# Weighing the second half of the heads as three fp32r products in an attention and mixture-of-experts kernel

## The reference, cut to what matters

```python
# x: (32, 128, 128), ctx_512: (32, 128, 64); 16 heads of width 64
qh = layernorm(x) @ Wq;  kh = ctx @ Wk;  vh = ctx @ Wv          # per head
attn = softmax(qh @ kh.T / 8)
x = x + tanh(g_xattn) * ((attn @ vh) joined over heads @ Wo + bo)
h = layernorm(x)
# 32 experts of width 64, 8 taken per token out of 2 of 4 groups, and a shared MLP
x = x + tanh(g_ffn) * (sum over taken experts of w * mlp_e(h) + mlp_shared(h))
```

## Time and profile before

| | |
|---|---|
| median of 3 runs | 668.14 us (667.93 to 668.69) |
| the profiled execution's own time | 665.33 us |
| its span | 663.5 us |
| PE busy | 649.6 us, 98% |
| DVE busy | 498.2 us, 75% |
| ACT busy | 365.1 us, 55% |
| POOL busy | 287.1 us, 43% |
| attention part | from the start to about 353 us |
| granted PE clock | full speed in all of the 40 slices |

### The profile page before, as it was taken

How to read it: one execution, slowest core, us unless ns; L and a number is a source line. 1 busy time by engine, 2 the same in 40 slices (tenths; PEclk the granted TensorE clock), 3 DMA queues, 4 the chain that set the end, 5 groups by cost and what they waited for, 6 DMA issues and landing times.

```text
span 663.5 us, 13627 instructions
## 1 busy us (share of the span) xinstructions
PE 649.6 (98%) x3668; PEld 472.3 (71%) x3668; DVE 498.2 (75%) x1330; ACT 365.1 (55%) x689; POOL 287.1 (43%) x317
## 2 busy tenths in 40 slices
PE   8999999999999999999999999999999999999997
PEld 5656666666666666676657878788887878788785
DVE  6989857767677775867786969968695977869564
ACT  3564556555465654656455555555655555555553
POOL 4222313233132331314302656566565656656654
PEclk9999999999999999999999999999999999999999
DMA  8323323232332323223226635272645535364640
GB/s 184 100 65 82 94 63 82 62 82 70 80 81 63 85 63 83 71 70 91 52 67 166 157 89 132 77 174 79 163 112 121 130 78 141 85 159 112 147 128 16
DMA packets 63244, 65.58 MB, mean 99 GB/s; under 512 B 26080, under 2 KB 41568, under 8 KB 63200
## 3 DMA queue, kind: packets, MB, share of 16 engines
q1 hardware_dynamic: 63200, 65.07, 39.4%
HBM read 61.64 MB, written 2.88 MB: 97 GB/s over the span
## 4 chain that ended last, share of the span: by engine, by line
PE 65%; DMA 9%; issue 8%; SPq 6%; DVE 6%; POOL 4%; ACT 1%; DVEq 0%; POOLq 0%; ACTq 0%
PE bank L1131 15%; PE bank L1132 14%; PE bank L1133 14%; PE bank L1207 7%; DMA inverse_bc<-inverse_dram 5%; POOL halves L501 4%; PE bank L1231 3%; PE bank L1167 3%; DMA inverse_dram<-inverse 2%; SPq L293 2%; PE bank L1187 2%; SPq L301 1%; DVE row_max L776 1%; DVE area L790 1%; PE bank L1196 1%
## 5 line engine op out<-in xcount | busy, mean ns | idle before, releaser
L501 POOL TENSOR_TENSOR halves<-area,halves 128x512 fp32r<-128x512 f32 x135 | 175.2, 1298 | 141.6 <-ACT halves L634 137.6
L647 ACT ACTIVATE area<-bank 128x512 f32<-128x512 f32 x136 | 81.4, 598 | 112.4 <-PE bank L1133 111.4
L587 ACT ACTIVATE area<-bank 128x512 f32<-128x512 f32 x128 | 69.5, 595 | 116.7 <-PE bank L1196 116.7
L1091 DVE TENSOR_TENSOR bank<-area,bank 128x512 f32<-128x512 f32 x128 | 88.5, 691 | 52.8 <-PE bank L1133 52.7
L1207 PE MATMUL bank<-area,ctx_keys 128*65 128x512 f32 (+1 forms) x256 | 124.7, 599 | 0.9 <-ACT u_odd L535 0.9
L1131 PE MATMUL bank<-x2t_hi,w_hi 128*128 128x512 f32 x272 | 110.1, 405 | 0.1
L1132 PE MATMUL bank<-x2t_hi,w_lo 128*128 128x512 f32 x272 | 107.1, 394 | 0.0
L1133 PE MATMUL bank<-x2t_lo,w_hi 128*128 128x512 f32 x272 | 106.2, 391 | 0.0
L447 POOL TENSOR_TENSOR ctx_hi<-ctx_raw,ones_col 128x128 fp32r<-128x128 f32 x32 | 20.4, 639 | 193.3 <-DMA ctx_raw<-ctx_t 193.3
L776 DVE TENSOR_REDUCE row_max<-bank 128x4 f32<-128x512 f32 x128 | 81.6, 679 | 25.8 <-PE bank L1167 21.5
L634 ACT ACTIVATE halves<-area 128x512 fp32r<-128x512 f32 x136 | 85.0, 626 | 16.8 <-DVE area L1099 16.3
(11 more groups left out here) (128 smaller groups left out, 1086.2 us busy)
## 6 DMA issues: line engine op xcount, KB each, us to landing
wbc<-rows_dram SPq DMA_DIRECT2D x128, 256.0 KB, 4.2
inverse_bc<-inverse_dram SPq DMA_DIRECT2D x64, 256.0 KB, 3.9
w_raw<-experts SPq DMA_DIRECT2D x32, 102.0 KB, 2.0
ctx_raw<-ctx_t SPq DMA_DIRECT2D x32, 64.0 KB, 1.8
ctx_keys<-ctx_nat SPq DMA_DIRECT2D x32, 64.0 KB, 2.0
out<-area SPq DMA_DIRECT2D x7, 256.0 KB, 3.9
max_rows<-max_t SPq DMA_DIRECT2D x64, 4.0 KB
area<-wq_t SPq DMA_DIRECT2D x1, 512.0 KB, 4.7
```

Of the source, the lines that this page charges most:

```text
L501: nc.gpsimd.tensor_tensor(hid_lo[:, u % SLOTS, :], hid[:, u % HIDS, :], raw(hid_hi[:, u % SLOTS, :]), ALU.subtract).then_inc(hidlo_ready, 1)
L587: nc.scalar.activation(probs_t[:, k, :, :], st_ps[q][:].rearrange("p (h n) -> p h n", h=4), ACT.Exp)\
L647: nc.scalar.activation(silu_g[:, u % 2, :], gate_ps[u % 2][:], ACT.Silu).then_inc(silu_ready, 1)
L1091: nc.vector.tensor_tensor(up_ps[u % UPS][:], silu_g[:, u % 2, :], up_ps[u % UPS][:], ALU.mult)\
```

## The change

In tiles t = 3 to 27 (25 of 32: the last tile of the first chunk and all of the loop) the two fp32 matmuls of half 1 are replaced by six fp32r matmuls of 512 columns on high and low halves. The halves come from new operations: ACT copies the exponentials of half 1 to `p_hi` (two operations of 128x512 a tile), DVE subtracts to form `p_lo` (two, both inputs in SBUF), POOL splits the context into `keys_hi` and `keys_lo` (128x192 each). They lie in tiles that are free in this time: `x2t_hi`, `x2t_lo` and the tails of `w_hi`, `w_lo`. DVE's part stands after `residual` and the statistics, ahead of `ln_apply`. In even steps ACT's part stands ahead of both `u_out` of half 0, in odd steps behind them.

```diff
+HALVED_FROM = CB - 1
+        p_hi = [x[:, 1, :] for x in (x2t_hi, x2t_lo)]
+        tail = slice(WCOLS - 2 * 3 * CD, WCOLS)
+        p_lo = [x[:, 0, :] for x in (x2t_hi, x2t_lo)]
+        keys_hi, keys_lo = (w[:, tail].rearrange("p (s n) -> p s n", s=2) for w in (w_hi, w_lo))
+        def halved_weights(b, first, last):
+            return not last and (not first or b == CB - 1)
 # POOL
+            def split_keys(b, t, c):
+                pool.wait_ge(keys_in[b], 16 * c + 16)
+                wait(pool, u_done, 4 * (t - 1) if not isinstance(t, int) or t > HALVED_FROM + 1 else 0)
+                nc.gpsimd.tensor_tensor(keys_hi[:, b % 2, :], ctx_keys[:, b, :], ones_col[:].broadcast_to([P, 3 * CD]),
+                                        ALU.mult).then_inc(keyshi_ready, 1)
+                pool.wait_ge(keyshi_ready, t + 1 - HALVED_FROM)
+                nc.gpsimd.tensor_tensor(keys_lo[:, b % 2, :], ctx_keys[:, b, :], raw(keys_hi[:, b % 2, :]), ALU.subtract)\
+                    .then_inc(keyslo_ready, 1)
...
+                    if halved_weights(b, first, last):
+                        split_keys(b, t, c)
                     split_weights(b % 2, t, 2 * c + b // 2, NB if last else t + CB)
 # ACT
+            def probs_high(t):
+                act.wait_ge(exp_ready, 4 * t + 4)
+                for q in range(2):
+                    nc.scalar.activation(p_hi[q], probs_t[:, 2 + q, :, :].rearrange("p h n -> p (h n)"), ACT.Copy)\
+                        .then_inc(phi_ready, 1)
...
+                    if b % 2 == 0 and halved_weights(b, first, last):
+                        probs_high(t)
                     u_out(t, b % 2, 0, 0)
                     if b % 2 == 1 and not last:
                         g_high(2 * c + 2 + b // 2, b // 2)
                     u_out(t, b % 2, 0, 1)
+                    if b % 2 == 1 and halved_weights(b, first, last):
+                        probs_high(t)
 # DVE
+            def probs_low(t):
+                for q in range(2):
+                    dve.wait_ge(phi_ready, 2 * (t - HALVED_FROM) + q + 1)
+                    nc.vector.tensor_tensor(p_lo[q], probs_t[:, 2 + q, :, :].rearrange("p h n -> p (h n)"),
+                                            raw(p_hi[q]), ALU.subtract).then_inc(plo_ready, 1)
...
+                        if h == 1 and halved_weights(b, first, last):
+                            probs_low(t)
                         if first:
                             for level in LN_AT.get(step_of_chunk, ()):
 # PE
+            def weigh_halves(t, b):
+                pe.wait_ge(keyslo_ready, t + 1 - HALVED_FROM)
+                for q in range(2):
+                    pe.wait_ge(phi_ready, 2 * (t - HALVED_FROM) + q + 1)
+                    wait(pe, u_ready, 4 * t + q + 1)
+                    cols = slice(0, CD + 1) if q == 0 else slice(CD, 3 * CD)
+                    ps = u_ps[q][0:CD + 1 if q == 0 else P, :]
+                    nc.tensor.matmul(ps, keys_hi[:, b % 2, cols], p_hi[q], start=True, stop=False)
+                    nc.tensor.matmul(ps, keys_lo[:, b % 2, cols], p_hi[q], start=False, stop=False)
+                for q in range(2):
+                    pe.wait_ge(plo_ready, 2 * (t - HALVED_FROM) + q + 1)
+                    cols = slice(0, CD + 1) if q == 0 else slice(CD, 3 * CD)
+                    nc.tensor.matmul(u_ps[q][0:CD + 1 if q == 0 else P, :], keys_hi[:, b % 2, cols], p_lo[q],
+                                     start=False, stop=True).then_inc(u_done, 1)
...
                     if started:
-                        for q in range(2):
-                            weigh(t - 1, (b - 1) % CB, 1, q, c + (b > 0))
+                        if halved_weights(b - 1, first, last) if b > 0 else not first:
+                            weigh_halves(t - 1, (b - 1) % CB)
+                        else:
+                            for q in range(2):
+                                weigh(t - 1, (b - 1) % CB, 1, q, c + (b > 0))
```

More of the change, by code:

```diff
@@ L203, in build @@
         st_done, exp_ready = sem("st_done"), sem("exp_ready")
+        phi_ready, plo_ready = sem("phi_ready"), sem("plo_ready")
+        keyshi_ready, keyslo_ready = sem("keyshi_ready"), sem("keyslo_ready")
         u_done, u_ready, inverse_ready = sem("u_done"), sem("u_ready"), sem("inverse_ready")
@@ L605, in attention @@
                     if last and b == 1:
+                        act.wait_ge(u_done, 4 * (NB - CB))
                         x2t_high(0, 0)
```

## The result

The changed kernel took 670.74 us (median of 8; 669.78 to 671.73), the kernel before 668.52 us beside it; ratio 1.0042, 95% interval 1.0029 to 1.0054. That is +2.8 us by the ratio and +2.2 by the medians: slower, and clear of the noise. The forecast was 670.3 us, +2.2.

A forecast was written before the change was run, and what follows sets the result against it. The prediction took the loop from one `g_project` to the next (g_low, scores, exponentials, SP, two DMAs, DVE) as the bound; 0 + 1.1 + 0.9 + 0.2 = +2.2 us on 668.14 gave 670.3 us, range 667.3 to 675.0.

The forecast's parts named there:

- PE's saving counted at 0: Half 1's products: 0.34 us saved a tile, 8.5 us in all, worth 0 because `g_project` waits for DVE's `row_max`.
- Place 1, into the last chunk: Tile 27's low halves stand ahead of DVE work without a pause from 312.94 to the end: +1.1 us.
- Place 2, into the loop: Subtractions of tiles 3 and 4 delay DVE and `xn` of chunk 2, so `g_project` comes later: +0.9 us.
- Place 3, `xn` in each chunk: At b = 0 the subtractions stand ahead of `ln_apply`, with POOL's work in the same stretch: +0.2 us in all.
- The margin of 0.5 us: At b = 0, `ln_apply` ends at 198.05 to 198.15 and may end as late as 198.61 before `g_project` suffers.
- The mis-sized term: DVE's two low-half subtractions of 512 columns, taken at 0.62 us each, 1.25 a tile.
- The long end that was kept, 1.27: DVE's subtraction at its other end: 1.27 us each, 2.54 a tile, from L1120, which ran beside a POOL operation.
- ACT and POOL at 0, SP at 0: ACT's copies and POOL's splits fit into idle time, SP's queue gets nothing new: each costs 0.
- A: Rival: PE was the bound all along; 661.6 us if the whole saving comes, 666 if only b = 3 periods; chance 0.12.
- B: Rival: low halves reach the loop's chain, `ln_apply` ends late and PE is 0.8 us late at b = 1; 676.3 us; chance 0.10.
- C: Rival: ACT's exponentials are late in odd steps, with only 0.24 us to spare; +3.6, 673.9 us; chance 0.10.
- D: Rival: the losses into the last chunk and into the loop are covered; 668.1 us; chance 0.16.

The follow-up runs named there:

- the shorter chain: Changed kernel without DVE's low subtractions (high halves read instead), and SP's store of the inverse sums issued ahead of the keys' load: 659.82 us, 0.9896.
- without b = 3: Changed kernel with DVE's low-half subtractions left out in steps b = 3 (tiles 3, 7, ... 27), high halves read instead: 667.53 us, 1.0007.
- second pair: Profiles of the kernel before and the changed kernel, both unchanged, run once more on one chip: 667.15 us (1.0007) and 670.28 us (1.0042).
- the split moved: Changed kernel with POOL splitting the context keys behind `split_weights` and `add_bias` instead of ahead of them: 669.91 us, 1.0042.
- the edit on SP: Kernel before with SP's store of the inverse sums issued ahead of the load of the keys: 662.76 us, 0.9929; on the changed kernel 666.36 us, 0.9986.

## Why the prediction was right

**PE's saving counted at 0.** Right, and shown by two runs: fp32 products in its place cost 0.4 us, within the noise, and without the subtractions the time is before's. A third, with the shorter chain, agrees: there the saving begins to count. The size was a little high: 0.34 us a tile said, 0.29 measured, since the six products take 1.51 us to the start of `project_out` and not 1.38. The forecast's picture of the waits was half right. PE would wait for `row_max` "as before", some 1.5 us a time, it said. That wait of the weight load is 0.8 us a time (9.8 in 12); in b = 1 the saving goes into the wait for `xn`. PE's idle time as a whole grew as said: span less busy time is 14.1 us in before's second profile and 22.1 in after's.

**Place 1, into the last chunk.** +1.1 said, +0.73 measured from the last `g_project` to the experts, +0.6 to +1.7 over all the profiles; without b = 3 it is gone. The step itself was as worked out: `invert` starts 12.70 us after the last `g_project` in before and 13.85 in after, 1.15 later, and DVE's pause for the DMA behind it is moved and not shortened (2.96 us and 3.00). In this pair 0.4 us of it is given back on the way to the experts.

**Place 2, into the loop.** +0.9 said, +1.48 measured, and this is where the sum was short. The subtractions of tiles 3 and 4 are both in it. From the start of the first to the next operation of DVE they take 62.24 - 60.72 = 1.52 us and 72.49 - 70.55 = 1.94, not 1.25, and `ln_apply` behind them 1.77, not 1.58.

**Place 3, `xn` in each chunk.** +0.2 said. The second pair has +0.56 over five chunks, but no run ties it to `xn`: without the subtractions of b = 0 these periods are no shorter. The margin of 0.5 us was there on paper, and DVE used it up: from the first subtraction to `ln_apply` 1.45 us go by and not 1.25, and `ln_apply` takes 1.95 us and not 1.58, with POOL at work in the same stretch. PE's 0.90 us wait has first to eat the saving and the old idle time, and it ends level with `row_max`. So a loss near nothing fits, and where the 0.56 come from is not shown.

**The mis-sized term** is then the subtraction, which was priced as if POOL were not there: 0.62 each was taken, from operations with one input in PSUM and from ones of 64 partitions. The rows of after by source line:

```profile
L820 DVE TENSOR_TENSOR x2t_hi<-area,x2t_hi x25: 655/691/1008, 60.7 to 316.1; 128x512 fp32r<-128x512 f32 x25
L820 DVE TENSOR_TENSOR x2t_lo<-area,x2t_lo x25: 683/942/1085, 61.4 to 316.7; 128x512 fp32r<-128x512 f32 x25
```

The first of a pair has a median of 0.69, the second one of 0.94. That POOL is the reason, two runs show, one from each side. With the keys split once the second subtraction's median is 0.69 (first row below); without the subtractions POOL's high halves of the keys (192 columns) have a median of 0.51 us (second row), and in after 0.95 (third):

```profile
L820 DVE TENSOR_TENSOR x2t_lo<-area,x2t_lo x25: 681/686/1017, 61.4 to 318.6; 128x512 fp32r<-128x512 f32 x25
L469 POOL TENSOR_TENSOR w_hi<-ctx_keys,ones_col x25: 498/508/1449, 49.6 to 301.5; 128x192 fp32r<-128x192 f32 x25
L469 POOL TENSOR_TENSOR w_hi<-ctx_keys,ones_col x25: 499/951/1527, 49.4 to 304.4; 128x192 fp32r<-128x192 f32 x25
```

That bears out the rule of the Trainium skill that was cited (SBUF — State Buffer, "Who interferes with whom"), in both directions. The long end that was kept, 1.27, is reached by no subtraction of the profiles (at most 1.09 in after, 1.11 with the split moved).

**ACT and POOL at 0, SP at 0.** Right as far as the runs tell: without the subtractions nothing is lost. POOL's part is not nothing beside them: it is in the longer subtractions, and may be worth the 0.7 us of the keys split once. In odd steps ACT had 0.24 us to spare by the forecast and has 0.19 in the trace:

```profile
210.89 0.62 ACT L618 ACTIVATE x2t_lo<-area 128x512 fp32r<-128x512 f32 x1
211.71 1.09 ACT L611 ACTIVATE area<-bank 128x512 f32<-128x512 f32 x2 [0.19 <-PE bank L1241]
```

**The rivals.** A is ruled out for the kernel as it stands, but was nearer than it looked: a chain shorter by 0.7 us a period makes PE the bound. B and C did not come about. D was wrong, places 1 and 2 were not covered. The sum was 2.2; in the second pair the three places gave 1.48 + 0.56 + 0.73 = 2.77. The total came out closer than its parts: in this pair place 2 was 0.6 too small and place 1 0.4 too large, and that they partly cancel is luck.

**Why the edit on SP gave 4.7 us and not 1 to 2.** Two numbers of that expectation were too small. In even steps the store is issued 0.39 us sooner after `invert` (0.48 to 0.09, means of 12), but SP then also issues the read back sooner after the store (1.98 to 1.70 us), so the chain is 0.67 us shorter, 8.1 in 12 periods. And PE's slack was read in one chunk, as 0.33 and 0.03 us; over the 12 `g_project` it is 3.3 and 4.2 us in the two profiles of before, and 0.6 with the edit. So the edit gave about what PE's slack allowed.

**Open.** How much of the 0.7 us of POOL's part is real: the interval of the run with the keys split once overlaps that of after. And the 0.56 us of chunks 2 to 6: the profiles of before differ by 1.1 us in the sum of the b = 3 periods (123.63 and 124.70), so a single period is no measure of slack at 0.1 us, nor one pair of profiles of a loss of half a us.

## What to carry to other kernels

An engine that is 98% busy may still be waiting once in each period, and then less work on it only makes that wait longer: before its work is cut, follow its waits at the one instruction per period where it is released, and ask what lies on the loop that releases it. A faster form of an operation that needs preparation on other engines is paid there; price that preparation at the places without a pause (the way into and out of a loop), not by the engine's average load. Where two chains are nearly level, shorten the one without arithmetic first: moving one DMA issue behind another gave 4.7 us, where 7.3 us less of matmul gave none. And when a wait is gone, see whether another has taken it over before it is called a gain.

## What was not expected of the hardware

One execution's profile can lie 2.8 us off the median of the same kernel (665.33 against 668.14 us), more than the change under study; a second profile of each kernel on one chip brought the two into line. And one 64 KB load ahead of an 8 KB store on SP's queue, 0.5 us of issue in half of the steps, was worth 4.7 us, 0.7% of the time; it also made the time from the store to the issue of the read back 0.28 us longer.
